# Attention's turned halves, its softmax division and the MLP's first products in a transformer kernel, rearranged

## The reference

```
x = x + attn_a(layernorm(x))
x = x + ffn(layernorm(x))
x = x + attn_b(layernorm(x))
x = x + ffn(layernorm(x))

# one of the two layers of ffn
h = shift_token(x)                       # features 64..127 come from the token before
q, k, v = split(h @ wqkv)                # 8 heads of 64
q, k = l2norm(q) * qs, l2norm(k) * ksc   # then a rotary turn with scales
o = softmax(q k^T, window of 64 and the one before, masked) @ v
x = x + o @ wo
h = layernorm(shift_token(x)) * lg + lb
a, g = split(h @ w1 + b1)                # 2 x 341
x = x + (a * gelu(g)) @ w2 + b2
```

## Time and profile before

| | us |
|---|---|
| median of 3 runs | 1001.57 |
| the profiled execution, whole | 1000.6 |
| its span | 998.5 |
| PE busy in the span | 939.0 |
| DVE busy | 732.4 |
| ACT busy | 728.0 |
| POOL busy | 386.4 |
| granted TensorE clock, mean | 0.996 of full speed |

### The profile page before, as it was taken

The page is one execution under the profiler, slowest core; times in us unless marked ns, Lnnn a source line. Parts: engine busy times, 40 slices in busy tenths (PEclk is TensorE's granted clock), DMA queues, the critical chain, the costliest instruction groups (busy, mean ns, idle before and its releaser), DMA issues.

```text
span 998.5 us, 22947 instructions
## 1 busy us (share of the span) xinstructions
PE 939.0 (94%) x8744; PEld 575.5 (58%) x8744; DVE 732.4 (73%) x1218; ACT 728.0 (73%) x1563; POOL 386.4 (39%) x272
## 2 busy tenths in 40 slices
PE   8999999999789999999999999999999999999985
PEld 4333333333566676666766566666666666766752
DVE  6887878886487777777777677777677777777741
ACT  3577777778688786877867677777778868788662
POOL 2110113123366536455443534434355454544411
PEclk9999999999999999999999999999999999999999
DMA  2210100000211101011000101000011011110100
GB/s 82 66 40 10 26 2 2 3 1 2 59 29 28 24 18 33 18 28 23 18 23 17 23 18 23 17 13 22 18 23 29 18 26 25 23 39 17 34 22 11
DMA packets 23303, 23.72 MB, mean 24 GB/s; under 512 B 8626, under 2 KB 15068, under 8 KB 23196
## 3 DMA queue, kind: packets, MB, share of 16 engines
q1 hardware_dynamic: 23196, 22.27, 9.3%
HBM read 6.16 MB, written 1.05 MB: 7 GB/s over the span
## 4 chain that ended last, share of the span: by engine, by line
PE 54%; DVE 10%; ACT 5%; issue 3%; POOL 1%; DVEq 0%; POOLq 0%; ACTq 0%
PE psum L1381 8%; PE psum L1350 6%; PE psum L1292 5%; PE psum L1389 4%; PE psum L1313 4%; PE psum L1302 3%; PE psum L1264 3%; PE psum L1253 3%; DVE BS L1619 3%; PE psum L1374 3%; PE psum L1255 3%; PE psum L1254 3%; DVE A L1615 3%; PE psum L1368 2%; PE psum L1277 2%
## 5 line engine op out<-in xcount | busy, mean ns | idle before, releaser
L1182 POOL TENSOR_TENSOR A<-A,BS 128x1024 f32<-128x1024 f32 x62 | 146.2, 2359 | 207.1 <-DVE BS L1619 206.9
L878 DVE TENSOR_REDUCE a_M<-psum 128x2 f32<-128x1024 f32 x128 | 155.3, 1220 | 34.0 <-PE psum L651 33.2
L1187 POOL TENSOR_TENSOR A<-A,RN 128x1024 f32<-128x1024 f32 x62 | 117.9, 1902 | 89.5 <-ACT RN L1511 86.0
L1496 ACT ACTIVATE f_PW<-psum,f_NM 128x128 f32<-128x128 f32 x512 | 138.5, 381 | 18.7 <-DVE f_NM L1651 18.7
L774 ACT ACTIVATE a_PT<-psum 128x1024 f32<-128x1024 f32 x128 | 128.8, 1020 | 23.2 <-PE psum L661 23.0
L1615 DVE TENSOR_TENSOR A<-psum,cos 128x512 f32<-128x512 f32 x124 | 84.8, 684 | 35.1 <-ACT SQ L1462 35.1
L1651 DVE TENSOR_REDUCE f_NM<-psum 128x4 f32<-128x512 f32 x128 | 82.1, 683 | 38.5 <-PE psum L1292 38.5
L1462 ACT ACTIVATE SQ<-psum 128x512 f32<-128x512 f32 x124 | 72.1, 624 | 49.4 <-PE psum L1255 46.4
L1381 PE MATMUL psum<-f_mid,w 128*128 128x512 f32 (+1 forms) x192 | 87.0, 603 | 2.7 <-DVE f_mid L1681 2.7
L1313 PEld LDWEIGHTS psum<-f_VS,f_PT 128*64 128x64 f32 x1024 | 64.5, 137 | 38.8 <-issue 38.3
L1619 DVE TENSOR_TENSOR BS<-psum,sin 128x512 f32<-128x512 f32 x124 | 84.2, 679 | 0.0
(11 more groups left out here) (212 smaller groups left out, 1946.1 us busy)
## 6 DMA issues: line engine op xcount, KB each, us to landing
f_VS<-V SPq DMA_DIRECT2D x112, 130.0 KB, 2.3
raw<-L_ffn_wqkv_dram SPq DMA_DIRECT2D x2, 768.0 KB, 4.8
...
```

What stands on the lines that cost most here:

```text
L878: nc.vector.tensor_reduce(M[:, quads % 2, t, 2 * j:2 * j + 2], psum[:, pair("scores", i), :], AX_X, ALU.max).then_inc(s("maxed"), 1)
L1182: nc.gpsimd.tensor_tensor(A[:, k % 2, :, :], A[:, k % 2, :, :], BS[:, k % 2, :, :], ALU.add)\
L1187: nc.gpsimd.tensor_tensor(x, x, RN[:, k % 2, :, None].to_broadcast([P, 2 * HW, DW]), ALU.mult)\
L1496: last = nc.scalar.activation(PW[:, u % 4, c, :], psum[:, bank("scores", u), P * c:P * c + P], ACT.Exp, bias=NM[:, u % 4, c:c + 1])
```

## The change

- **Both halves by VectorE.** DVE's stage `turn_p` (lag 3, first after `lead`) copies both turned halves; ACT's copy (L1518) is gone.
- **Division ahead of the turn.** A new stage `weigh` (lag 2): DVE sums the exponentials of both halves (128x1024 to 128x8) and takes reciprocals of the 8 sums; POOL multiplies PW by them (128x1024). `turn_p` on PE waits for that (`weighed`), moves from lag 2 to lag 3, and stands first in PE's step. VS and V lose the ones column.
- **Sums turned.** `sums` (lag 3, right behind `turn`) now has V and VS as the stationary operand and PT as the moving one, 64 columns, and gives the transposed output in one bank. `turn_o` (4 transposes for a tile), its two reciprocals and its two products on DVE go; ACT copies `sums` to OT.
- **w1 in three products.** Each of the six products of a group becomes three float32r ones (w1_h*mid_h, w1_h*mid_l, w1_l*mid_h). ACT and POOL split w1 once (128x1364, steps 4 and 5). DVE writes mid_h and mid_l (one instruction more for a group).
- **Moved.** On DVE the norms' ends `var_*` and `w2` go one step later (lags 5, 4, 8, 11 and 7) and to the step's head, behind the copies; `store` goes one step later. PE takes `turn_p` ahead of `project`. `gates` shares memory with w1, OF and OUT with `raw`; ln_squared is also scratch for the MLP's input. wo is laid out plainly and loaded by one DMA for a layer.

```diff
-           ("turn_o", 3, of_tile), ("project_b", 10, of_sequence), ("w1", 5, of_group), ("turn_p", 2, of_tile), ("turn_p_2", 2, of_tile),
+    "PE": [("turn_p", 3, of_tile), ("turn_p_2", 3, of_tile),
@@ pool
+                    elif stage == "weigh":
+                        k = i
+                        pool.wait_ge(s("den_recip"), k + 1)
+                        x = PW[:, 2 * (k % 2):2 * (k % 2) + 2, :, :].rearrange("p u c x -> p (u c) x")
+                        nc.gpsimd.tensor_tensor(x, x, RD[:, k % 2, :, None].to_broadcast([P, 2 * PAIRS, P]), ALU.mult)\
+                            .then_inc(s("weighed"), 1)
@@ tensor
-                    pe.wait_ge(s("exped"), u + 1)
+                    pe.wait_ge(s("weighed"), u // 2 + 1)
...
+                                    dst[DW * j:DW * j + DW, c, WIN * w:WIN * w + WIN],
+                                    values[:, k % 4, 2 * c + j, :],
+                                    PT[:, (2 * k + j) % 4, c, WIN * w:WIN * w + WIN], start=True, stop=True)
...
-                                nc.tensor.matmul(take(kind, 3 * i + blk)[0:w, :],
-                                                 w1[:, layer, first + lo:first + lo + w],
-                                                 mid[:, :], start=True, stop=True).then_inc(s(kind), 1)
+                                nc.tensor.matmul(dst, w1_h[:, layer, of], mid_h[:, :], start=True, stop=False)
+                                nc.tensor.matmul(dst, w1_h[:, layer, of], mid_l[:, :], start=False, stop=False)
+                                nc.tensor.matmul(dst, w1_l[:, layer, of], mid_h[:, :], start=False, stop=True)\
+                                  .then_inc(s(kind), 1)
@@ vector
-                            nc.vector.reciprocal(RD[:, u % 4, :], x[:, :, DW]).then_inc(s("den_recip"), 1)
...
-                            nc.vector.tensor_tensor(ON[:, u % 4, :, :], x[:, :, 0:DW],
...
+                        dve.wait_ge(s("exped"), 2 * k + 2)
...
+                        nc.vector.tensor_reduce(RD[:, k % 2, :], x, AX_X, ALU.add).then_inc(s("den"), 1)
+                        dve.wait_ge(s("den"), k + 1)
+                        nc.vector.reciprocal(RD[:, k % 2, :], RD[:, k % 2, :]).then_inc(s("den_recip"), 1)
...
+                            nc.vector.scalar_tensor_tensor(out=mid_l[:, :], in0=ln_squared[:, :],
+                                                           scalar=vecs[:, layer, 1:2], in1=mid_h[:, :].bitcast(F32),
+                                                           op0=ALU.add, op1=ALU.subtract).then_inc(s("ln_done"), 1)
```

174 lines of the change are left out of this document (82 added, 92 removed).

## The result

The changed kernel takes 1011.76 us, the median of 4 runs (1009.97 to 1014.73), against 1001.54 of the kernel before on the same chip: 1.0103 times as long, 95% interval 1.0078 to 1.0129. Forecast were 974.4 us and a range of 955 to 991, so the sign was wrong too. The profiled execution took 1009.97 us, its span is 1007.9.

What follows compares the result with a forecast made beforehand. PE was taken to bound the kernel, with DVE the next limit. Ordinary groups -23.6, beside attention B +2.4, start -4 and end -2 sum to -27.2 us: from 1001.57 to 974.4, range 955 to 991.

Steps and rivals of the forecast that it cites:

- The sum for the ordinary group: Groups without attention B: PE work 38.0 plus 1.2 idle gives 39.2 us, 2.55 gained each, -23.6 over 9.25 groups.
- The clock's price: On PE: a fall of the granted clock like the one at 255 to 260 costs 1.7 us.
- the signs listed for "wrong": Long waits of `turn_p` for POOL or copies for PE, `sums` over 1.1, mid_l over 0.8, clock under 1.00 beside attention B.
- Beside attention B: Four groups: PE work 49.0, waits 3.4 at `center_y`, 2.3 in w1 step, 0.2 more: 54.9 us each, +2.4 in all.
- rival D: Beside attention B: longer PE waits bring the clock down, one fall a group, +7 us, 981; chance 0.10.
- Start and end: Steps 2 to 9: -4 us, with 2 taken as lost (bounds 0 to 4), POOL splitting w1; the end: -2.
- The rule of the Trainium skill: At mid_l: two-SBUF-input DVE and SBUF-reading GpSimd instructions block each other, a reduce does not; 30 us possible, 0 taken.
- C: DVE's chain keeps most of its idle time: ordinary groups 43.0 us, attention B's 55.9, total 1014; chance 0.08.
- B: Ordinary groups: DVE's waits at `weigh` add up and DVE leads, 40.2 us a group, total 987; chance 0.17.

Runs made afterwards that it cites:

- e2: Changed kernel with the ends of norms b and y on DVE put back in their own step, behind `tokens_b`: 998.12 us, 0.9957 of the kernel before.
- e14: Kernel before with `latent` moved behind `project` on PE and `squares` on ACT, and `var_y`'s end at the head of DVE's next step: 1030.41 us.
- e3: Changed kernel with 12 added matmuls that PE runs into `center_y`'s bank before waiting for X: 1006.11 us, 1.0033 of the kernel before.
- e1: Changed kernel with POOL's list reordered, `weigh` first, `split_w1` last and a step later: 1008.72 us, 1.0058 of the kernel before.
- e10: Changed kernel with the edits of e1, e2 and e6, `latent` back at the step's head on PE and ACT, `lead`'s casts on ACT: 983.15 us.
- e6: Changed kernel with `center_y` moved behind `scores` and `var_y` behind `w2` on PE: 998.24 us, 0.9974 of the kernel before.

## Why the prediction was wrong

**What was right.** The sum for the ordinary group: DVE busy 36.10 (36.5), POOL 28.18 (28.3), the group 39.10 (39.2). PE is busy 38.40 (38.0) and idle 0.70 (1.2), two misses that nearly cancel. `sums` takes 1.08 us from start to start before and after, as priced. Nine groups gave the -23.6 that was forecast for 9.25. w1 takes 4.13 us and 0.23 more for its last product, 4.4 (4.3), `weigh`'s two instructions 1.21 and 0.20 us, and PE's wait at `center_y` 2.97 (3.2 to 3.6). The clock's price, 1.7 us a fall, held for all eight falls up to the end of attention B. Of the signs listed for "wrong", two came: `turn_p` waiting for POOL's product, and a clock under 1.00 beside attention B.

**Step 1 that failed: "Beside attention B", the term that isn't there.** The sum 49.0 + 3.4 + 2.3 + 0.2 has no entry for the ends of the norms b and y. I followed what the later ends do to DVE's chain and asked only of the MLP norm whose bank they hold. The banks of `center_y` and `center_b` cost PE 2.28 + 1.01 us a group, 13.2 us for the four, before what the clock adds. The forecast had +2.4 us there; the stretch grew by 27.0, 18.5 of it without the clock's share. e2 gave 14.6 us back by undoing these ends alone, and e14 shows `var_y`'s end at 11.0 in another kernel. With the ends back and the clock's loss taken off, the group is 54.7, and the sum said 54.9. That is closer than its terms: PE waits 2.97 us at `center_y` (3.4), 1.69 in the w1 step (2.3) and 1.0 elsewhere (0.2).

**Step 2: the granted clock, priced right and counted wrong.** The forecast took no fall beside attention B and gave rival D (one a group, +7 us) a chance of 0.10. There were five, 8.5 us, and three more in steps 2 to 8. The row to have followed was my own: a wait of 3.2 to 3.6 us, about twice the longest one that had left the clock at 1.00 (1.8 us, at POOL's scaling). e3 gave 7.0 us back by filling the wait.

**Step 3: "Start and end", split of w1 0 to 4 us.** I bounded it by the length of `split_w1`. What cost was what stands behind a waiting instruction: `split` waits 4.40 us for ScalarE with `weigh` queued behind it, and PE then waits 3.10 and 3.20 us, each with a fall of the clock; a third wait, 2.60 us at step 8, has one too, behind `lead`'s casts on VectorE (2.50 us, 0.84 before). By the start of step 9 the changed kernel was 6.8 us later, not 4 earlier. e1 gave 4.5 us back, and e10 another 4.7 for the casts of `lead`.

The misses add up: 24.6 in attention B, 10.8 up to step 9, 1.1 at the end, together 36.5 of the 36.6 us between -27.2 and +9.4.

**The rule of the Trainium skill.** I used half of it. The Trainium skill, "SBUF — State Buffer", section "Who interferes with whom", says besides that a copy, a cast or a tensor_scalar of VectorE can enter modes in which it contends with GpSimd for a port pair that they share, and that whoever issues first has the pair for the whole instruction while the other is blocked. The trace agrees: the earlier trace rows had the 985 ns, and the four instances so long all lie beside a GpSimd operation, as here in the kernel before:

```profile
531.18 0.98 DVE L1681 TENSOR_SCALAR f_mid<-f_mid,vecs 128x512 f32<-128x512 f32 x1
...
530.61 1.27 POOL L1219 TENSOR_TENSOR f_QB<-f_QB,f_NEG 128x512 f32<-128x512 f32 x1
```

GpSimd starts first and ends at 531.88, and VectorE ends 0.28 us later. `mid_l`, the one with two SBUF inputs on which I spent the paragraph, took 0.75 us all 16 times and never lay beside GpSimd, so that half stays untested.

**The rivals.** None of the five had the ends of the norms. D had the falls of the clock beside attention B, but on top of a forecast that lacks the waits for the norms' banks, at 981. C came near the number (1014) by letting VectorE lead the ordinary groups, which 39.10 us rules out; B is ruled out by the same row.

**Left open.** Why the clock falls behind one wait and not behind its like: in the changed kernel three of the four waits of 2.97 us had a fall behind them, in e2 all four, and there twice as long. Nor is the wait's length enough: falls came behind waits of 1.28 us in e6, and the one at 708 us in the changed kernel has no wait longer than 1.0 us in the 20 us ahead of it.
